# Attention, GRU scan and mixture-of-experts layer on one core: shared chunks first, routing in pieces, down projection up to ten chunks behind

## What is computed

```python
x = x + attention(interpolate(x, cond), wq, wk, wv, wo)      # B=4, S=512, D=512
# GRU over 512 time steps, batch 4: cell(h, x)
gi = x @ W_ih + b_ih;  gh = h @ W_hh + b_hh
r = sigmoid(i_r + h_r); z = sigmoid(i_z + h_z); n = tanh(i_n + r * h_n)
h_new = (1.0 - z) * n + z * h
# mixture of experts on the 2048 states: E=16 experts of 352 units, shared one of 704
scores = sigmoid(xf @ gate_w.T); topv, topi = top_k(scores, 2)
topv = topv / topv.sum(-1)
def mlp(x, w1, w2, w3): return (silu(x @ w1.T) * (x @ w3.T)) @ w2.T
y = mlp(xf, sw1, sw2, sw3) + sum(mlp(xf, w1[e], w2[e], w3[e]) * weight[:, e])
return x + y
```

## Time and profile before

| | us |
|---|---|
| median of 3 runs (lowest, highest) | 3007.75 (3006.93, 3011.0) |
| the profiled execution, its own time | 3008.64 |
| its span, first to last instruction | 3006.8 |
| PE busy in the span | 2679.4 (89%) |
| DVE busy | 2183.7 (73%) |
| ACT busy | 1056.4 (35%) |
| POOL busy | 1231.2 (41%) |

### The profile page before, as it was taken

How to read it: one execution, slowest core, us unless ns; L and a number is a source line. 1 busy time by engine, 2 the same in 40 slices (tenths; PEclk the granted TensorE clock), 3 DMA queues, 4 the chain that set the end, 5 groups by cost and what they waited for, 6 DMA issues and landing times.

```text
span 3006.8 us, 158572 instructions
## 1 busy us (share of the span) xinstructions
PE 2679.4 (89%) x69122; PEld 1975.4 (66%) x69122; DVE 2183.7 (73%) x7136; ACT 1056.4 (35%) x3485; POOL 1231.2 (41%) x2955
## 2 busy tenths in 40 slices
PE   5599898987899899899989998998999899899999
PEld 2344343433555677777777777777777777777788
DVE  4667666571566788888888888888888888888832
ACT  3452636261122233333333333333333333333333
POOL 0441312021222355455545544544555455455544
PEclk9599999998899999999999999999999999999999
DMA  4102010102210224323332432243243224322244
GB/s 168 60 2 47 3 33 13 26 20 56 41 14 4 62 81 89 89 80 85 88 88 80 93 83 84 83 91 86 83 92 88 80 81 91 88 82 83 81 140 134
DMA packets 271431, 215.83 MB, mean 72 GB/s; under 512 B 162576, under 2 KB 214032, under 8 KB 270352
## 3 DMA queue, kind: packets, MB, share of 16 engines
q1 hardware_dynamic: 269584, 201.49, 25.5%
q10 hardware_dynamic: 1152, 4.19, 0.3%
HBM read 188.85 MB, written 16.78 MB: 68 GB/s over the span
## 4 chain that ended last, share of the span: by engine, by line
PE 38%; DVE 27%; issue 5%; ACT 3%; POOL 1%; DMA 1%; DVEq 0%; SPq 0%; POOLq 0%; ACTq 0%
PE ps L1034 25%; PE ps L1056 7%; DVE h L945 6%; DVE turn_n L930 4%; DVE turn L933 4%; PE ps L1069 4%; DVE npre L936 4%; ACT cand L841 3%; DVE fresh L942 3%; DVE hcur L944 3%; DVE hcur L947 2%; PE ps L1045 1%; DMA gi<-gi_scratch 0%; POOL hid L779 0%; DMA w<-in_w 0%
## 5 line engine op out<-in xcount | busy, mean ns | idle before, releaser
L1034 PE MATMUL ps<-whh,hcur 128*32 128x128 f16 x49152 | 790.7, 221 | 168.7 <-DVE hcur L947 143.5
L1034 PEld LDWEIGHTS ps<-whh,hcur 128*32 128x32 f16 x49152 | 699.2, 97 | 319.1 <-DVE hcur L947 285.4
L1056 PE MATMUL ps<-hb,w 128*128 128x256 f16 x6400 | 812.6, 274 | 2.5 <-issue 2.0
L1056 PEld LDWEIGHTS ps<-hb,w 128*128 128x128 bf16 x6400 | 605.8, 98 | 103.4 <-issue 6.2
L834 ACT ACTIVATE r<-ur 128x16 f32<-128x16 f32 x512 | 110.6, 216 | 1007.3 <-DVE ur L924 1007.3
L1069 PE MATMUL ps<-hid,w 128*128 128x256 f16 x3200 | 435.4, 273 | 14.9 <-POOL hid L779 14.9
L779 POOL TENSOR_TENSOR hid<-hidf,hid 128x256 f16<-128x256 f32 x400 | 268.6, 671 | 346.6 <-ACT hid L830 346.6
L767 POOL TENSOR_TENSOR hidf<-up 128x256 f32<-128x256 f32 x400 | 292.9, 732 | 169.1 <-DVE up L915 151.6
L1069 PEld LDWEIGHTS ps<-hid,w 128*128 128x128 bf16 x3200 | 298.5, 98 | 69.4 <-issue 18.7
L759 POOL COPY hb<-hcur 128x32 f16<-128x32 f16 x512 | 170.5, 333 | 320.6 <-DVE hcur L947 320.6
L921 DVE STREAM_TRANSPOSE turn<-ps 128x128 f32<-128x128 f32 x512 | 162.3, 317 | 172.9 <-PE ps L1034 161.3
(11 more groups left out here) (139 smaller groups left out, 3333.7 us busy)
## 6 DMA issues: line engine op xcount, KB each, us to landing
w<-in_w SPq DMA_DIRECT2D x400, 256.0 KB, 2.7
w<-in_w SPq DMA_DIRECT2D x400, 128.0 KB, 2.4
gi_scratch<-stage SPq DMA_DIRECT2D x48, 256.0 KB, 2.6
gi<-gi_scratch SPq DMA_DIRECT2D x16, 768.0 KB, 9.4
x2T<-in_xT SPq DMA_DIRECT2D x4, 1024.0 KB, 7.6
out<-xo ACTq DMA_DIRECT2D x8, 512.0 KB, 3.1
stage<-in_W_hh SPq DMA_DIRECT2D x1, 3072.0 KB, 10.9
x2T<-in_W_ih SPq DMA_DIRECT2D x1, 3072.0 KB, 11.8
```

The lines of the kernel that those rows point to most:

```text
L1034: mm = pe.matmul(ps[j * COLS:(j + 1) * COLS, bank, 0:P], hcur[:, k], whh[:, s, k, at:at + P], start=(k + s == 0), stop=(k == KT - 1 and s ...
L1056: mm = pe.matmul(ps[:, UB[u], w * TOK:(w + 1) * TOK], w13[:, u, w, k], hb[:, f % 2, s, k].rearrange("p b t -> p (b t)"), start=(w + k + s ...
```

## The change

- Chunk order: the shared expert's units come first (`SCH = 6` chunks, then 44 routed ones, still 50). They need no routing weights, so `weigh` and `share` run for `NWG = 22` pairs and not 25; for a shared chunk ACT copies the second up product to SBUF (in `sigmoid`) and DVE does only L917's product.
- PE's filler starts at once in each block. `UPS` and `DOWNS` give the units done by each step: all 64 steps have some, the weight matmuls are counted in, and at most 10 units of two matmuls stand in a step (49 steps have 10; the others 9 in 13 steps, 8 in one and 7 in one).
- `down` lags `up` by up to ten chunks and a bit; ten hidden buffers, twelve buffers for `w2`. Of each block 32 down units (eight chunks) are left to the first nine steps of the next (`LEFT`), or to the tail. The zeroing matmuls into the output banks go.
- Routing: 16 instructions over steps 1 to 6 (`ROUTE`: 4, 2, 2, 2, 4, 2), the turned weights at step 7 (`TURN`), `result` at step 9. Logits and turned weights use bank `WB`.
- The gate inputs of a block come in one transfer of contiguous rows into one of two buffers, a block ahead, where two half-block transfers with short rows were.
- POOL: `low_half` stands behind `copy_states`. ACT: z before 1-z, and DVE's `zh` waits for z alone.

```diff
+SCH = -(-SI // P)
+NCH = SCH + E * TOPI // P
+NWG = (NCH - SCH) // 2
-HIDS, AHEAD = 3, 3
-UP, DOWN, FIRST = 8, 4, 3
-GI_AT = 30
+HIDS, W2S = 10, 12
+UP, DOWN = 8, 4
+GI_AT = 20
...
+        TURN, RESULT, EXPERTS = 7, 9, 10
+        ROUTE = {1: 4, 2: 2, 3: 2, 4: 2, 5: 4, 6: 2}
+        GATE = [2, 3, 4, 6, 7, 8] + [EXPERTS + n * (TB - EXPERTS) // (NCH - SCH) for n in range(NCH - SCH)]
+        WEIGH = [GATE[SCH + 2 * p] - 1 for p in range(NWG)]
+        LEFT = [4, 3, 4, 4, 3, 5, 4, 3, 2]
+        LATE = sum(LEFT)
+        UPS = [3, 10, 16, 22, 29, 34, 40, 46, 53, 60]
+        DOWNS = [0] * EXPERTS
+        for i in range(EXPERTS, TB):
+            ups = -(-(UP * NCH - UPS[EXPERTS - 1]) * (i - EXPERTS + 1) // (TB - EXPERTS - 1)) + UPS[EXPERTS - 1]
+            UPS.append(min(ups, UP * NCH, UP * gated(i - 1) + 2 * UP))
+            shares = sum(1 for at in WEIGH if EXPERTS <= at <= i)
+            total = UP * NCH - UPS[EXPERTS - 1] + DOWN * NCH - LATE + NWG - 1
+            downs = -(-total * (i - EXPERTS + 1) // (TB - EXPERTS)) - (UPS[i] - UPS[EXPERTS - 1]) - shares
+            DOWNS.append(max(DOWNS[-1], min(downs, DOWN * NCH - LATE)))
...
+            def gi_load(blk):
+                need(sp, h_ready, (blk - 1) * TB + 1 if blk > 1 else 0)
+                sp.dma_start(gi[:, blk % 2], gi_dram[blk]).then_inc(gi_in[blk % 2], 16)
...
-                need(sp, down_done, n - 1)
+                need(sp, down_done, n - W2S + 1)
...
+                    copy_states(blk, i)
                     if f >= 0 and i > 0:
                         for c in gate_at[i - 1]:
                             low_half(f, c)
-                    if f >= 1 and i == 0:
-                        for c in gate_at[TB - 1]:
-                            low_half(f - 1, c)
-                    copy_states(blk, i)
...
+                if c < SCH:
+                    need(act, hidf_done, n)
+                    nc.scalar.copy(up2[:], ps[:, UB[c % 2], TOK:2 * TOK]).then_inc(up2_done, 1)
...
-                nc.scalar.activation(omz[:], uz[:], ACT.Sigmoid, scale=-1.0).then_inc(z_ready, 1)
                 nc.scalar.activation(z[:], uz[:], ACT.Sigmoid).then_inc(z_ready, 1)
+                nc.scalar.activation(omz[:], uz[:], ACT.Sigmoid, scale=-1.0).then_inc(z_ready, 1)
...
-                dve.wait_ge(z_ready, 2 * g + 2)
+                dve.wait_ge(z_ready, 2 * g + 1)
                 nc.vector.tensor_tensor(zh[:], z[:], h[:], ALU.mult).then_inc(kept, 1)
                 dve.wait_ge(kept, g + 1)
+                dve.wait_ge(z_ready, 2 * g + 2)
...
-                        if i == 1:
-                            route_tokens(f)
-                            if f >= 1:
-                                result(f - 1)
-                        if i == 2:
+                            routing = route_tokens(f)
+                        for _ in range(ROUTE.get(i, 0)):
+                            next(routing)
+                        if i == TURN + 1:
                             weights_low(f)
+                        if i == RESULT and f >= 1:
+                            result(f - 1)
...
+                    if i == TURN:
                         turn_weights(f)
+                    for p in weigh_at[i]:
+                        weigh(f, p)
+                    take(ups, UPS[i] - (UPS[i - 1] if i else 0))
+                    if i < len(LEFT) and f >= 1:
+                        take(downs, LEFT[i])
+                    if i >= EXPERTS:
+                        take(downs, DOWNS[i] - DOWNS[i - 1])
             f = NBLK - 1
...
+            take(ups, UP)
+            take(downs, LATE)
+            take(ups, UP)
             turn_weights(f)
...
```

More of the change, by code:

```diff
@@ L669, in need @@
                 eng.wait_ge(sem, count)
-        NINIT = 4
+        NINIT = 3
         GI_HALF = TB // 2
[L674 to L685, removed]
@@ new lines, in scan_and_ffn, with gated @@
+        ROUTE = {1: 4, 2: 2, 3: 2, 4: 2, 5: 4, 6: 2}
+        GATE = [2, 3, 4, 6, 7, 8] + [EXPERTS + n * (TB - EXPERTS) // (NCH - SCH) for n in range(NCH - SCH)]
+        WEIGH = [GATE[SCH + 2 * p] - 1 for p in range(NWG)]
+        gate_at = [[c for c in range(NCH) if GATE[c] == i] for i in range(TB)]
+        weigh_at = [[p for p in range(NWG) if WEIGH[p] == i] for i in range(TB)]
+        LEFT = [4, 3, 4, 4, 3, 5, 4, 3, 2]
+        LATE = sum(LEFT)
+        def gated(i):
+            return sum(1 for at in GATE if at <= i)
@@ L696, in scan_and_ffn @@
+        for c in range(NCH):
+            assert UP * (c + 1) <= UPS[GATE[c]] and GATE[c] < TB - 1
+        for i in range(TB):
+            assert UPS[i] <= UP * gated(i - 1) + 2 * UP and DOWNS[i] <= DOWN * gated(i - 2)
+        assert DOWNS[-1] == DOWN * NCH - LATE
         block = ctx.enter_context(nc.Block())
@@ L881, in _ @@
             score_experts(f)
[L882 to L885, removed]
             for c in range(NCH):
-                if c % 2 == 0:
-                    share(f, c // 2)
+                if c >= SCH and c % 2 == 0:
+                    share(f, (c - SCH) // 2)
                 sigmoid(f, c)
@@ L1014, in _ @@
             take_logits(f)
-            route_tokens(f)
+            for _ in route_tokens(f):
+                pass
+            gate_chunk(f, 0)
+            gate_chunk(f, 1)
             result(f - 1)
             weights_low(f)
-            for c in range(NCH):
+            for c in range(2, NCH):
                 gate_chunk(f, c)
@@ L1073, in down, with all_ups, all_downs, take @@
                     yield
-            def feed(f):
+            def all_ups(f):
                 for c in range(NCH):
-                    if c % 2 == 0 and c:
-                        weigh(f, c // 2)
                     yield from up(f, c)
-                    if c >= 2:
-                        yield from down(f, c - 2)
+            def all_downs():
+                for f in range(NBLK):
+                    for c in range(NCH):
+                        yield from down(f, c)
+            def take(units, count):
+                for _ in range(count):
+                    next(units)
             def logits(f):
                 pe.wait_ge(copied, (f + 1) * TB + CREDIT)
-                need(pe, up1_done, f * NCH)
+                need(pe, wsb_done, f * NWG)
                 for t in range(2):
```

170 lines of the change are left out of this document (76 added, 94 removed).

## The result

The changed kernel takes 2842.4 us (median; 2840.4 to 2845.3), the kernel before 3009.4 in the same comparison: ratio 0.9446, 95% interval 0.9429 to 0.9462. The prediction was 2814 in a range of 2785 to 2852; the time is inside, 28 us above the point. One of the four executions of experiment 2's kernel took 5294.7 us, its matmuls far longer throughout (a mean of 439 ns for one of `up`, where 274 is usual) and for a reason that stays open; the other three took 2916.7 to 2918.6, and the ratio given there is theirs.

The account below looks back on a forecast made before the run. PE was to bound 20-matmul steps at 3.74 us, the dependent chain others at 3.60. Start 995.3, blocks 1664, gate inputs 3 and tail 150.6 gave a span of 2813, median 2814 us, range 2785 to 2852.

Parts of the forecast that it names:

- The step: Scan steps of a block: 49 PE-bound at 3.74 us, 15 chain-bound at 3.60, together 237.3 us a block.
- POOL's chain later by 0.24 us: In chunk steps, products and z sum come 0.24 us late; 0.1 absorbed, 0.14 left, which vanishes in PE-bound steps.
- Routing, result, late halves: Per block: 0.3 us for routing pieces and result on DVE, 0.3 for high halves waiting on a buffer's down.
- Gate inputs: Scan breaks while the larger transfer is in flight: between 0 and 2.1 us a block, 0.5 taken for six, 3 us.
- if scans break on "issue": PE's scan: one of the listed signs that would show the prediction wrong; no size given.
- Tail: After the last state: 5.2 us more down matmuls, partly filling idle PE, 0.7 less weight matmuls; together unchanged at 150.6 us.
- small allowances: In the seven blocks: 0.3 and 0.3 us a block for routing, result and late halves, less 1.3 in the first.
- start: Time until block 1's steps begin: unchanged at 995.3 us.
- POOL's chain (2850 to 2878): Rival for the scan steps: the z sum, not PE, sets the step; 37 us more, up to 64; chance 0.10.
- Chain alone: Rival for the scan steps: longer runs hide PE's 0.14 us, 48 us less, 2766; chance 0.06.
- Contention moved: Rival for chunk steps: the low half holds DVE as long in its new place, 126 us more, 2940; chance 0.06.
- The clock: Rival for the scan: granted clock falls from 2.4 to 1.2 GHz for a large part, 3.4 us a step; chance 0.02.

Follow-up runs that it names:

- experiment 2: The kernel before with only GpSimd's low half moved behind the copy of the states: 2917.8 us, ratio 0.9691.
- experiment 6: The changed kernel with the down product of the high half alone, 4 matmuls a chunk in place of 8: 2787.2 us, ratio 0.9259.
- experiment 1: The changed kernel with GpSimd's low half put back before the copy of the states: 2955.7 us, ratio 0.9821.
- experiment 4: The changed kernel without loads of gate inputs for blocks 2 to 7, which read block 1's again: 2825.8 us, ratio 0.9384.
- experiment 9: The changed kernel with gate inputs in twelve pieces and also a block's output sent in four pieces: 2829.9 us.
- Experiments 3, 4 and 5: The changed kernel with gate inputs in twelve pieces (2829.9 us), not loaded after block 1 (2825.8), or as two short-row transfers (2874.1).

## Why the prediction was right, and where its 28 us went

- **The step.** Right. It said 49 steps of 3.74 and 15 of 3.60 a block, 237.3. Taken as in experiment 2 (at each step the second shortest of seven blocks), the changed kernel's block is 237.4 us. The held state update is gone (169 ns), the first ten steps of a block stay under 4.1 us, PE bounds the 20-matmul steps (experiment 6), and undoing the move brings the hold back (experiment 1).
- **POOL's chain later by 0.24 us.** Mis-sized, without effect. The prediction let the low half start when the copy's row ends; it starts 0.17 us after the copy's row begins, so products start 1.07 us after the state and not 1.24, and the z sum moves by at most some 0.1. Experiment 6 shows that nothing of this reaches the step.
- **Routing, result, late halves: 0.6 a block.** Too much: 237.4 a block leaves 0.1 for them. Of the two instructions of step 5 that were to be held beside a low half, one is, for 0.67 us in all seven blocks, and PE's 3.74 covers it; the other (L989) takes 0.17:

```profile
L986 DVE TENSOR_TENSOR best<-best 128x2 f32<-128x2 f32 x7 | 4.7, 673 | 0.0
```

- **Gate inputs: 3 us in all.** This is the term that failed, and by the prediction's own sign ("if scans break on "issue"") it is wrong. It measured 16.6 (experiment 4), 2.8 a block, above even the 2.1 that the prediction gave as the most. The prediction had the mechanism's row, a scan broken on "issue" while such a transfer was in flight, and took 0.5 a block; it did not reckon that with PE at its bound nothing makes up for a break, nor that the clock falls after some of them (5 of the 16.6 us, by the estimate in experiment 4). The long breaks stand at steps 27 to 29 of blocks 1 to 6, those with a transfer in flight, and not in block 7, which has none.
- **The rest.** Beside that transfer, steps longer than in their sister blocks add up to the difference of 1697.4 and 7 × 237.4 = 1662, 35 us, less 16.6: about 19 us, spread over many steps, the longest at step 12. The prediction had no such term, though the kernel before shows 14 us by the same count. They are there without the gate inputs (experiment 4 has 19 us too), and sending the output in pieces did not lessen them (experiment 9). Their cause was not found.
- **Tail.** 150.6 predicted, 151.5 measured.
- **Sum.** Breaks, with the slow matmuls after them, 35.4 us where 3 were counted, +32.4; the small allowances of 2.9 of which 0.9 is seen, −2.0; start −0.7; tail +0.9: 2812.9 becomes 2843.5, the span measured. The median lies 1.1 below that span where the prediction put it 0.9 above its own, hence 28 and not 30. That the time lies in the range owes something to luck: it is 10 us under the top, and with the gate inputs at the prediction's own worst, 2.1 a block in six blocks, its sum would have been 2824. What filled the range was breaks that it did not reckon.
- **Rivals.** POOL's chain (2850 to 2878): refuted by experiment 6, though the time lies near it. Chain alone (2766): refuted, 3.74 in the trace. Contention moved: refuted, L918 takes 0.42 us beside the low half, as in the earlier trace rows. The clock: for a large part of the scan, as the rival had it, refuted: the granted clock of the blocks is 1.00 in their window, the upper level. But this mean hides three stretches of 3.4 us at 0.50, and they came after stops of PE and not for want of them.

## To carry to other kernels

When two engines share something, look at which instruction of a group is longer than its twin of the same size: here 0.50 us in a chain of 4.10, whose cure was to place GpSimd's instruction where VectorE reads PSUM. Such a move pays more if the consumers are given slack (buffers, a longer lag) and PE's work is spread evenly: 113 us here against 91. And once PE has no idle time, every break of it is paid in full: cut a large transfer into pieces between those it must not delay (12.5 us here). A mean granted clock of 1.00 over a long window can hide short stretches at the lower level; look for them after each long stop of PE.

## What was not expected of the hardware

PE's instructions are themselves brought by DMA, and while a large transfer was in flight they came late. Queue 8 carries instructions in pieces of 16 KB (543 in all, 8.90 MB). DMA in the changed kernel from 1088.5 to 1095.5, while the gate inputs were in flight (there is no row of queue 8), and from 1148 to 1155 without them:

```profile
DMA packets 398, 1.75 MB, mean 249 GB/s; under 512 B 32, under 2 KB 160, under 8 KB 288
q1 hardware_dynamic: 398, 1.75, 68.0%
```
```profile
q1 hardware_dynamic: 572, 0.78, 34.8%
q8 instruction: 1, 0.02, 1.0%
```

From 1088.5 to 1095.5 no piece of instructions began, where in the blocks 78% of them come 3.5 to 4.5 us after the last; at 1095.68 PE stopped in the middle of a scan for 2.41 us with nothing to wait for but "issue". It is so in all six blocks with a transfer: the next piece begins 7.0 to 8.4 us after the last, and within 1 us of its start PE stops for 1.4 to 2.4 us. The longest stop elsewhere, 1.20 us at 1765.67, also follows a gap of 8.1 us, with a block's output in flight. But 17 other gaps of more than 6 us passed without a stop of over 0.4, so a late piece alone is not enough. Experiments 3, 4 and 5 (pieces, none, short rows) show that the long breaks come from the transfer; that the late piece is what stopped PE is read from this timing, not shown by itself. The Trainium skill (Runtime: NRT & Kernel Launch, section "Instruction fetch mechanics") describes a small instruction store per engine, refilled in blocks of 16 KiB over a DMA queue of its own; the trace agrees with the size.

Two instructions in a row on POOL overlap in the profile: L786's row begins at 2085.23 while L766's runs from 2085.06 to 2085.39. An estimate that lays POOL's rows end to end is too long.
